# Four attention blocks on one core: two heads per row maximum and exponential, other layer 0 statistics, the last value product taken first

## The reference

```python
xr   = x.reshape(B, 32, 4, 256)                      # group norm: 32 groups of 4 channels
h    = (xr - mean) * rsqrt(var + EPS[l]) * gn_w + gn_b   # mean, var over (4, 256)
q, k, v = wq @ h + bq, wk @ h + bk, wv @ h + bv      # 128 x 128 weights
attn = softmax(q.T @ k * scale)                      # over keys, 256 x 256
x    = wp @ (attn @ v) + bp + x
```

## Time and profile before

| | us |
|---|---|
| median of three runs | 98.39 |
| the profiled execution | 98.5 |
| its span, first to last instruction | 96.7 |
| TensorE matmul busy, of the span | 88.9 (92%) |
| TensorE weight load busy | 67.8 (70%) |
| VectorE busy | 69.7 (72%) |
| ScalarE busy | 55.1 (57%) |
| GpSimd busy | 13.9 (14%) |

### The profile page before, as it was taken

The page is one execution under the profiler, slowest core; times in us unless marked ns, Lnnn a source line. Parts: engine busy times, 40 slices in busy tenths (PEclk is TensorE's granted clock), DMA queues, the critical chain, the costliest instruction groups (busy, mean ns, idle before and its releaser), DMA issues.

```text
span 96.7 us, 2489 instructions
## 1 busy us (share of the span) xinstructions
PE 88.9 (92%) x946; PEld 67.8 (70%) x946; DVE 69.7 (72%) x187; ACT 55.1 (57%) x123; POOL 13.9 (14%) x31
## 2 busy tenths in 40 slices
PE   5999998999799899999899998999989999999990
PEld 5999697866555578697566557979855646778670
DVE  0476899696753799969593379997878337777870
ACT  3203555977894612695859851339786983046810
POOL 7322241000002222020200204202020000220000
PEclk9999999999999999999999999999999999999999
DMA  2982000000000000000000000000000000000002
GB/s 31 327 305 106 0 0 7 0 3 7 0 0 0 0 7 0 3 0 0 7 0 0 7 0 0 0 0 7 0 0 0 7 0 0 0 3 0 7 26 83
DMA packets 1739, 2.28 MB, mean 24 GB/s; under 512 B 320, under 2 KB 1216, under 8 KB 1728
## 3 DMA queue, kind: packets, MB, share of 16 engines
q1 hardware_dynamic: 1440, 1.97, 6.8%
q10 hardware_dynamic: 288, 0.16, 0.5%
HBM read 1.86 MB, written 0.26 MB: 22 GB/s over the span
## 4 chain that ended last, share of the span: by engine, by line
PE 82%; DVE 7%; ACT 6%; issue 2%; ACTq 0%
PE ps L540 12%; PE ps L506 12%; PE ps L607 12%; PE ps L563 9%; PE ps L595 8%; PE ps L644 5%; PE ps L550 4%; PE ps L578 3%; PE ps L629 3%; PE ps L529 2%; ACT probs L696 2%; PE ps L571 2%; PE ps L518 2%; PE ps L520 2%; PE ps L581 2%
## 5 line engine op out<-in xcount | busy, mean ns | idle before, releaser
L789 DVE TENSOR_REDUCE neg_max<-ps 128x2 fp32r<-128x512 f32 x48 | 30.4, 683 | 4.2 <-PE ps L563 4.2
L696 ACT ACTIVATE probs<-ps 128x512 f32<-128x512 f32 x48 | 25.4, 606 | 3.0 <-PE ps L595 3.0
L506 PE MATMUL ps<-blank 128*128 128x128 f32 x80 | 14.4, 317 | 1.1 <-DVE blank L724 1.0
L506 PEld LDWEIGHTS ps<-blank 128*128 128x128 f32 x80 | 12.2, 219 | 2.0 <-DVE blank L724 1.0
L667 ACT ACTIVATE q_low<-ps,bias_low,const 128x256 fp32r<-128x256 f32 x12 | 6.5, 565 | 11.7 <-PE ps L540 11.7
L607 PE MATMUL ps<-probs,v_heads 128*32 128x256 f32 x192 | 12.8, 385 | 0.0
L540 PE MATMUL ps<-hn,ws 128*128 128x256 f32 x40 | 11.6, 397 | 0.0
L452 POOL TENSOR_SCALAR k_ext<-k_low,const 128x256 fp32r<-128x256 f32 x12 | 6.7, 556 | 28.4 <-DVE k_low L773 28.4
L456 POOL TENSOR_TENSOR grp<-grp,const 128x1 f32<-128x1 f32 x8 | 4.5, 566 | 42.1 <-DVE grp L742 42.1
L563 PE MATMUL ps<-k_high,q_split 32*128 32x256 f32 x96 | 7.6, 327 | 1.0 <-ACT probs L696 0.8
L672 ACT ACTIVATE k_high<-ps,bias 128x256 fp32r<-128x256 f32 x12 | 5.5, 474 | 4.9 <-PE ps L540 2.9
(11 more groups left out here) (76 smaller groups left out, 144.1 us busy)
## 6 DMA issues: line engine op xcount, KB each, us to landing
w<-in_w SPq DMA_DIRECT2D x3, 384.0 KB, 5.4
xs<-in_x SPq DMA_DIRECT2D x2, 128.0 KB, 3.1
w<-in_w SPq DMA_DIRECT2D x1, 256.0 KB, 6.1
out<-xs SPq DMA_DIRECT2D x4, 64.0 KB, 1.6
const<-in_constants ACTq DMA_DIRECT2D x1, 136.0 KB, 3.0
vec<-in_vectors ACTq DMA_DIRECT2D x1, 16.0 KB, 3.7
```

The costliest lines, as they stand in the source:

```text
L506: mm(slot(*step)[:, 0:C], blank[:, :], blank[:, :], start=True, stop=True)
L696: nc.scalar.activation(probs[b][:, i, :, :].rearrange("p c t -> p (c t)"), slot("scores_t", l, b, i // PACK, i % PACK)[:, :], ACT.Exp, sca ...
L789: nc.vector.tensor_reduce(neg_max[b][:, i // PER, :, QUAD * (i % PER) + MAX_ROW], slot("scores", l, b, i // PACK, i % PACK)[:, :].rearrang ...
```

## The change

- `MERGE = 2`: a row maximum (layers 0 to 2) reads the two neighbouring banks of two heads, 128 by 1024, in one instruction, and so does an exponential. 24 and 24 instructions stand where there were 48 and 48. PSUM is one tensor of 8 banks, and scores and transposed scores get their banks in aligned pairs (0-1, 2-3, 4-5, 6-7); a pair counts as free when both are. A step that needs one bank takes one from the pair that comes free last (`choose_banks`).
- Statistics: x stands in a wider tile, with a column of sqrt(256 * EPS) on either side. The squares' pass takes 257 columns, so EPS comes with it, and the matmul L512 is gone in all layers. In layer 0 the sum of x is taken on ScalarE (a copy with an accumulator and a small instruction that negates it), beside the squares on VectorE; the three moments go through one matmul. Also in layer 0, x less the mean times the weight is made (`centre`) while GpSimd works on the power, and `normalise` is one instruction. The negated averaging matrix is made on GpSimd behind the second power, not ahead of the first.
- Loads: the identity is its own tensor, loaded by SyncE behind w0, and the two matrices made from it are a step of their own (`selectors`), needed first by the first turn of maxima. The vectors stand within the constants (164 columns). ScalarE issues x1.
- Layer 3: v is projected with its bias, kept as channels by tokens (`store_v`), and multiplied by wp at once (`project_u`, `store_u`). The product with the probabilities is then the projected output, and the residual reads it. The steps value bias and projection (L784, L644) go from both halves of both batches. The second half of each batch is written by ScalarE's queue.
- The planner has other costs, due numbers and landing times, and `ENOUGH`, the share of each window that TensorE is to be active, is .5 and not .46.

```diff
+def choose_banks(holders, done, wanted, start):
+    late = float("inf")
+    free = [0. if not h else done.get(h[-1][1], late) for h in holders]
+    runs = [max(free[n:n + MERGE]) for n in range(0, BANKS, MERGE)]
+    if wanted > 1:
+        first = sorted((at, n) for n, at in enumerate(runs))[:wanted // MERGE]
+        if first[-1][0] == late:
+            return None
+        return max(start, first[-1][0]), [MERGE * n + j for _, n in first for j in range(MERGE)]
+    if wanted == 1:
+        start = max(start, min(free))
...
+        return start, [min((-runs[n // MERGE], n) for n, at in enumerate(free) if at <= start)[1]]
...
-            sp.dma_start(xs[1][:, :], x[1]).then_inc(x_in[1], 16)
+            sp.dma_start(ident, eye).then_inc(ident_landed, 16)
...
-                    mm(m[:, 0:3], group_avg, const[:, EPS_COL + 3 * l:EPS_COL + 3 * (l + 1)], start=True, stop=False)
...
+                        mm(m[:, 0:3], group_avg, mom[b][:, :], start=True, stop=True).then_inc(means_done, 1)
+                    else:
+                        pe.wait_ge(minus_avg_ready, 1)
+                        pe.wait_ge(x_ready, nth("residual", l - 1, b))
+                        mm(m[:, 0:1], minus_avg[:, :], mom[b][:, 1:2], start=True, stop=True)
                         pe.wait_ge(moments_done, nth("moments", l, b))
+                        mm(m[:, 1:3], group_avg, mom[b][:, 1:3], start=True, stop=True).then_inc(means_done, 1)
...
+                elif kind == "project_u":
+                    pe.wait_ge(v_stored, nth("store_v", l, b))
+                    bank_free(step)
                     for n in range(NCH):
+                        last = mm(slot(*step)[:, n * C:(n + 1) * C], v_one[b][:, n * CHUNK:(n + 1) * CHUNK],
+                                  w[l][:, W_P[l], :], start=True, stop=True)
+                    last.then_inc(u_projected, 1)
...
             act.dma_start(const[:, :], constants).then_inc(const_in, 16)
-            act.dma_start(vec[:, :, :], vectors).then_inc(vec_in, 16)
+            act.dma_start(xs[1], x[1]).then_inc(x_in[1], 16)
...
+                if kind == "sum_x":
+                    act.wait_ge(x_in[b], 16)
+                    nc.scalar.activation(x_copy[b][:, :], xs[b], ACT.Copy,
+                                         accum_out=mom[b][:, 1:2]).then_inc(x_summed, 1)
+                    act.wait_ge(x_summed, nth("sum_x", l, b))
+                    nc.scalar.activation(mom[b][:, 0:1], mom[b][:, 1:2], ACT.Copy, scale=-1.0).then_inc(sums_ready, 1)
...
-                    nc.scalar.activation(probs[b][:, i, :, :].rearrange("p c t -> p (c t)"),
-                                         slot("scores_t", l, b, i // PACK, i % PACK)[:, :], ACT.Exp,
+                    nc.scalar.activation(probs[b][:, MERGE * i:MERGE * (i + 1), :, :].rearrange("p h c t -> p (h c t)"),
+                                         run("scores_t", l, b, i).rearrange("p h t -> p (h t)"), ACT.Exp,
...
+                elif kind == "centre":
+                    m = slot("group_means", l, b)
+                    ts(centred[b][:, :], xs[b], m[:, 1:2], vec[:, l, GN_W:GN_W + 1], ALU.subtract,
+                       ALU.mult).then_inc(x_centred, 1)
...
+                    n, first = divmod(MERGE * i, PER)
+                    dst = neg_max[b][:, n, :, :].rearrange("p c (j e) -> p j c e", e=QUAD)
+                    nc.vector.tensor_reduce(dst[:, first:first + MERGE, :, MAX_ROW],
+                                            run("scores", l, b, i).rearrange("p h (c t) -> p h c t", c=NCH),
...
                 elif kind == "residual":
-                    dve.wait_ge(out_projected, nth("project_out", l, b, i))
...
+                    dve.wait_ge(attended, nth("attend", l, b, i))
+                    tokens = slice(i * CHUNK, (i + 1) * CHUNK)
+                    stt(out=xs[b][:, tokens], in0=slot("attend", l, b, i)[:, 0:CHUNK], scalar=vec[:, l, BP:BP + 1],
+                        in1=xs[b][:, tokens], op0=ALU.add, op1=ALU.add).then_inc(x_ready, 1)
```

More of the change, by code:

```diff
@@ L55 @@
 }
[L56 removed]
+FIRST_STEPS = {"moments": ("V", .47, .6), "add_bias": ("V", .35, .5)}
 ONE_HEAD_STEPS = {
@@ L60 @@
     "turn_p": ("P", .25, .45), "store_p": ("A", .32, .5), "attend": ("P", .45, .65),
-    "store_attended": ("V", .29, .45), "project_out": ("P", .25, .45), "residual": ("V", .29, .45),
+    "store_v": ("A", .47, .65), "project_u": ("P", .45, .65), "store_u": ("A", .32, .5),
+    "residual": ("V", .29, .45),
     "write": ("S", .1, 2.),
@@ new lines @@
+    "turn_back": (2339, 2931, 4717, 5805, 7329, 7809),
+    "store_attended": (2384, 2976, 4762, 5904, 7374, 7854),
+    "project_out": (2444, 3036, 4822, 5985, 7457, 7914),
+    "residual": (2514, 3106, 4892, 6058, 7527, 7984, 8650, 8790, 8904, 8965),
+    "scale_w": (2066, 4366, 6653),
+    "fold_bias": (1151, 4494, 6661),
+    "scale_q": (8081, 8411),
+    "round": (8072, 8414),
+    "project_u": (8184, 8675),
+    "store_u": (8249, 8740),
+    "turn_p": (8437, 8517, 8744, 8805),
+    "store_p": (8482, 8562, 8789, 8850),
@@ L175, in step_needs @@
             step("normalise", 0, ("rsqrt", 0))
+            if l == 0:
+                needs["group_means", l, b, 0].append(("sum_x", l, b, 0))
+                step("centre", 0, ("variance", 0))
+                needs["normalise", l, b, 0].append(("centre", l, b, 0))
             sets = SETS if l < MULTI else 1
@@ L211, in step_needs @@
                     needs[kind, l, b, 0] = [needs[kind, l, b, 0][0], ("add_bias", l, 0, 0)]
+                needs["store_v", l, b, 0].append(("add_bias", l, 0, 0))
+                step("project_u", 0, ("store_v", 0))
+                step("store_u", 0, ("project_u", 0))
                 for qc in range(NCH):
-                    chain = ["scores", "row_max", "exps", "divide", "turn_p", "store_p", "attend", "store_attended",
-                             "project_out", "residual", "write"]
+                    chain = ["scores", "row_max", "exps", "divide", "turn_p", "store_p", "attend", "residual", "write"]
                     for kind, before in zip(chain, ["round"] + chain):
@@ L708, in _ @@
                                          ACT.Copy).then_inc(p_stored, 1)
+                elif kind == "write" and i == 1:
+                    act.wait_ge(x_ready, nth("residual", l, b, i))
+                    act.dma_start(out[b][:, CHUNK:T], xs[b][:, CHUNK:T]).then_inc(out_written, 16)
                 elif kind == "store_out":
```

304 lines of the change are left out of this document (154 added, 150 removed).

## The result

The changed kernel took 102.39, 102.40, 103.22 and 103.53 us: median 102.81. It is slower, by a ratio of 1.0458 (95% interval 1.0335 to 1.0581). The prediction said 95.4 and gave slower 1 chance in 20. The profiled execution took 102.39 us with a span of 100.6, so again 1.8 lie outside it.

A forecast was written before the change was run, and what follows sets the result against it. One dependent chain bounds both ends; a mixture of VectorE's maxima, ScalarE's exponentials and steps between bounds the middle. Start -1.8, end -1.2, L512 -0.4, merge -1.5 and +1.8 sum to -3.1: 98.5 becomes 95.4, range 93.8 to 97.4.

The forecast's parts named there:

- The start: Layer 0 up to the first scores: new statistics and projection order shorten the dependent chain, -1.8 us.
- batch 1 gains more than batch 0, because its x is issued one slot sooner: Layer 0's start: batch 1 therefore doesn't take back batch 0's gain; no cost charged.
- k0 was to come second: Layer 0's projections: k0 second of four instead of third, first scores 0.43 us earlier.
- The merge, engine time: Row maxima and exponentials over two banks save 3.1 us of engine time; half counted, -1.5.
- The merge, waits: Score steps: waits for paired banks 1.5 us, short steps behind longer maxima 0.3; +1.8 in all.
- The rival that an instruction over two banks takes as long as two: Merged maxima and exponentials: the 1.5 us saving is missing, time 96.9; chance 0.06.
- the slower rival: TensorE waits for a pair's second bank at scores, 0.3 us at each of 24 steps: 101.1; chance 0.05.
- head start lost: Layer 2: batch 1's statistics behind batch 0's second pack cost four maxima, +1.8 us net, 97.2; chance 0.26.
- the very sign that I had named for being wrong: Batch 1 reaching layer 3 less than 1.5 us earlier would show the forecast wrong.
- L512: Matmul removed from the chain, counted six times in layers 1 to 3: 0.3 to 1.0 us, taken as -0.4.
- The end: Layer 3's end: residual waits for the last product alone and another projection goes, -1.2 us.
- The -0.22 for the other half's projection: Layer 3: the projection standing ahead of the last product goes, saving 0.22 us.

The follow-up runs named there:

- e9: Changed kernel with single maxima and exponentials (MERGE = 1) in the new ranks, packs' banks still in aligned pairs; 103.07 and 100.50 us.
- e5: Changed kernel with three zero matmuls moved from behind batch 1's first averaging to ahead of it, one added ahead of batch 0's; ratio 1.0153.
- e8: Kernel before without the eight zero matmuls between first averaging and first projection; 100.70 to 102.31 us, ratio 1.0291.
- e3: Kernel before with only the new layer 3 (project_u, store_u); 97.78, 101.45, 101.65 and 101.74 us.
- e1: Changed kernel with each merged instruction issued as two of one bank, order and banks kept; 102.89 to 104.62 us, ratio 1.0454.
- e6: Changed kernel with MERGE = 1, x1's landing time corrected, shared steps at the kernel before's ranks, ENOUGH .46; 97.49, 98.22, 100.02 and 100.04 us.
- e4: Changed kernel planned with MERGE = 1: single maxima and exponentials, free banks, new ranks; 101.57 to 102.34 us, ratio 1.0331.
- e14: Changed kernel with x1 issued by SyncE behind w0; 102.77 and 102.25 us, ratio 1.0413.

## Why the prediction was wrong

The prediction had -3.1 and the traces have +4.1 up to the last residual. Of the 7.2 us between them the start has 2.6, the middle 3.65, and the end with batch 1's lag 1.0.

**The start** (-1.8 forecast, +0.78 measured). The step that failed is "batch 1 gains more than batch 0, because its x is issued one slot sooner". I had it as a gain and never asked what stands behind it. Issued at 1.16 and not 1.63, x1 landed no earlier (5.50, before 5.08), not at the planner's 3.8, and batch 1's sums, averaging and squares stand ahead of batch 0's variance or projections in the fixed lists of three engines. The tile came 3.87 behind x where I had 2.78: 1.1 us. The second failure is unspoken: I took the projections' 1.73 as given, but that is their price at the higher pace. In the changed kernel, whose TensorE idles twice, they cost 1.1 more; that its gaps keep the pace low is what e9's trace shows for a longer gap, and what e5 and e8 make likely. The third is the order: k0 was to come second and save 0.43, but all four projections (the fourth is batch 1's first q) and two more zero matmuls stand ahead of the first scores, so nothing of it showed. Against a long execution, e3's, the changed kernel's first scores are 2.8 earlier (14.37 and 11.59), more than forecast. Against a short one they are 0.8 later.

**The merge, engine time** (-1.5 forecast, -1.14 in e1's middle). Right. Two maxima end to end, and two exponentials:

```profile
12.39 2.36 DVE L866 TENSOR_REDUCE neg_max<-ps 128x4 fp32r<-128x1024 f32 x2
```

```profile
41.33 1.94 ACT L769 ACTIVATE probs<-ps 128x1024 f32<-128x1024 f32 x2 [0.44 <-PE ps L659]
```

A merged maximum comes every 2.36 - 1.22 = 1.14 us where two took 1.194, and a merged exponential every 1.94 - 1.023 = 0.917 where two took 0.986. The saving is 0.054 and 0.069 a pair, 24 of each 3.0 us; I had 3.1. The Trainium skill's "VectorE: DVE Perf Modes" (The TRN2 errata) would have 6.4. The trace speaks for the row. The rival that an instruction over two banks takes as long as two is ruled out.

**The merge, waits** (+1.8 forecast). e9 and e1 give 1.2 for the pairs and 0.8 for one step in place of two: 2.0, of which layers 1 and 2 show 1.0. The size was about right, but not the view I named for it. TensorE's waits for the exponentials' banks are 0.7 in sum at the scores (0.8 before) and 0.7 at one projection. The plan knows the pairs and can order the work around a missing one, so most of the price would lie in the order; that is argued, not shown. It depends on the ranks: in the earlier ones the pairs cost 3.9, half of what the slower rival gave them. That rival got the side right by luck. The waits of TensorE that it was made of didn't come, and the pairs are little more than a quarter of the loss.

**The ranks** (costed at nothing, except as a rival). This is the step that failed in the middle, and its largest term, +2.0. ScalarE's wait for transposed scores goes with it: 3.0 before, 3.3 in e6, but 7.4 in e4 and 8.3 in e9 and in the changed kernel. The rival "head start lost" named layer 2 and the right four maxima and gave them 1.8; 1.3 was found. I made it a rival with 0.26, on the ground that batch 0's gain comes back to batch 1 later. It wasn't so: batch 1 reaches layer 3 at 88.82, where it was 84.17, the very sign that I had named for being wrong. The diff gave the new ranks in figures, so their price belonged in the sum.

**L512** (-0.4 forecast). Not seen. At equal ranks the middle is 0.65 longer, not shorter (e6 against before), 0.48 of it in layers 1 and 2. What costs it stays open; the new rule for single banks, which came with the change, was not tried by itself.

**The end** (-1.2 forecast, -0.53 measured, and 0.32 of that given back by batch 1's lag). The residual's 0.95 went. The -0.22 for the other half's projection didn't come, and the last product ends 0.42 later than before. I had looked for cover on ScalarE, where `store_u` (95.94 to 96.33) does end before the stored probabilities are there. In e3 the engine without room was TensorE: the first probabilities were divided at 94.84, but their turn began at 95.29, behind `project_u` and batch 0's second product, 0.45 each. In the changed kernel the same turn began at 95.92. `project_u` had ended just then, but the divided probabilities came no sooner than 95.86, because VectorE's reciprocal had stood 0.3 behind batch 0's residual (95.05). Which of the two binds there isn't separated. The new layer 3 alone (e3) is worth 0.37 up to the residual, and about 0.7 by its times.

**Summed**: start +0.8, new ranks +2.0, the merge +0.9 in net, the rest that is new +0.65, lag and end -0.2: 4.1.

## What to carry to other kernels

Where each engine walks one fixed list, a load that lands late holds the work of everyone behind it; check every landing time that a plan assumes against the trace before costing what comes after. Due numbers can cost more than the instructions they serve (2.0 against a saving of 1.1 here), and what they cost depends on the rule for the banks: change one at a time. And at the start of a short kernel a gap on TensorE is not priced by its length alone, but also by what the matmuls after it then cost.

## What the runs showed of the hardware

- One row maximum over two banks takes 1221 ns and one exponential 1023 ns, with no jump at the bank's edge: 1.05 ns a column more than 512 columns for VectorE (683) and 0.81 for ScalarE (606).
- The same steps at the start, without a gap on TensorE, show the low pace until 5.2 us or until 12.8, at 98.4 or 102 us (the kernel before and e3). With gaps of 0.6 to 1.3 us in the first 7 us none of eight executions (four of the changed kernel, four of e8) was short; with most of that gap time filled, four of six lay near 100. What sets the moment in a gapless one stays open.
- After an idle stretch of 1.84 us the granted clock fell back to one half, from 7.9 to 11.3 us, though it had risen at 4.5 (e9): eight projections took 3.63 us for 1.89.
- A load of 128 KB (x1), with x0 (128 KB), w0 (256 KB) and the constants under way, took 3.45 us in the kernel before, 3.7 to 4.7 from ScalarE's queue in 12 traces, and 4.2 from SyncE's in e14.
